# The causal triangle of an attention kernel, added by VectorE where TensorE added it with matmuls

## The chip, the cores and the metric

One NeuronCore of one Trainium2 chip runs the whole program; the seven other cores are idle. The metric is the device time of one execution in microseconds (us). The kernel before takes 2070.18 us, the median of three runs (2068.84 to 2073.34).

## What is computed

The reference passes eight sequences of 512 tokens with 256 channels through two layers. Layer one is a local attention (44 fixed offsets for each token), layer two a causal attention, and a mixture of experts follows each. Only the causal attention is touched by the change. Cut to what matters:

```python
Q = split_heads(x @ Wq + bq)      # 16 heads of 16 channels
K = split_heads(x @ Wk + bk)
V = split_heads(x @ Wv + bv)
scores = jnp.einsum('bhqd,bhkd->bhqk', Q, K) / jnp.sqrt(jnp.float32(D_HEAD))
causal = jnp.tril(jnp.ones((T, T), dtype=bool))
scores = jnp.where(causal, scores, -jnp.inf)
attn = jax.nn.softmax(scores, axis=-1)
out = jnp.einsum('bhqk,bhkd->bhqd', attn, V)
```

## The kernel before, in words

**Calls and the planner.** The work is cut into calls: A (local attention of one sequence), B (causal attention of one sequence) and F (experts, sixteen calls). A and B calls alternate after the first two A, and each F call runs beside the attention call after its own. Every call is a list of phases, and a phase is a list of blocks, each on one engine with a cost in us and needs (`local_phases`, `causal_phases`, `expert_phases`, L127 to L279). `ordered` (L391) is a list scheduler that runs when the kernel is built: it always takes the block that can start first, and the one with the longest way behind it where two tie. The result is a fixed order of instructions for each of the five engines, and `play` (L501) writes it out. A block is never broken up by another. So a changed cost or a new block in `causal_phases` can change the order of everything.

**Banks.** PSUM has eight banks. A and B calls share banks 0 to 3 in rotation and bank 4 for sums that are held; F calls rotate through banks 5 to 7. A fill may start when the reader of the fill before it in that bank is done (`fills_of` L365, `bank_free` L737).

**A causal call.** Q and K are each split into three bf16 parts that are stacked along the contraction (`q_st`, `k_st`, 96 rows), so that one bf16 matmul gives the scores. This takes a write to DRAM and a read back ("stacks"). Then, for each of the 16 heads:

- *Raw scores, S* (`raw_scores` L1596). Three fills hold four query tiles i of 128 queries: i = 3 (512 keys), i = 2 and i = 0 (384 and 128 keys), i = 1 (256 keys). For each tile TensorE multiplies q by k (L1603) and then adds the triangle of the diagonal block with a 128-column matmul of the identity and `causal` (L1605). VectorE takes the negated maximum of each tile with a `tensor_reduce` (L1287): 64 tiles in a call, 512 in all. After eight heads `mx` (L1295 to L1298) splits the maxima in three bf16 parts, `mT` turns them, and they go through DRAM into rows 96 to 98 of `q_st`.
- *Turned scores, ST* (`turned_scores` L1609). Four heads make a group, and a step is one of its four key tiles k. TensorE multiplies k by q with the maxima subtracted (L1619, 512, 384, 256 or 128 columns), then adds the turned triangle to the first 128 of these columns with a matmul of the identity and `causal_T` (L1621). `SHARE` (L75) says how heads share a bank: one head in a fill for k = 0 and 1, two for k = 2, four for k = 3, so 44 fills in a call, 352 in all, and 64 triangle matmuls in a call, 512 in all. ScalarE reads each fill with one exponential (L1050) into `p_T`, which holds two steps, so the exponential of step n waits for PV of step n-2.
- *PV* (`weigh_values` L1625, L1638) multiplies the exponentials with the values and a column of ones.

In the order of `causal_phases` the maxima of the first eight heads and two more heads come ahead of any ST. The S fills of the other six heads are laced with the ST fills of the first six steps. The other ST steps stand alone on the attention side.

```python
nc.tensor.matmul(ps[:, at:at + (i + 1) * P], q_st[0:K, h, i * P:(i + 1) * P],
                 k_st[0:K, h, 0:(i + 1) * P], start=True, stop=False, skip_group_check=True)
ins = nc.tensor.matmul(ps[:, at + i * P:at + (i + 1) * P], ident_b[:], causal[:],
                       start=False, stop=True, skip_group_check=True)
```

**Engines in the same queue.** VectorE also makes the 88 products of every A call (L1231), norms (stats, L1163 to L1170; xn, L1176), the ranking of the experts (L1317 to L1346), the sums of the experts (L1373, L1378) and the close of an F call (L1395, L1400). ScalarE also reads the expert matmuls (L1085, L1069, L1102).

## Time and profile before

| | before |
|---|---|
| median of three runs | 2070.18 us |
| the profiled execution | 2066.49 us |
| its span, first to last instruction | 2064.5 us |
| mean granted TensorE clock | 0.939 of 2.4 GHz |
| PE busy (modelled) | 1770.7 us, 86% |
| VectorE (DVE) busy | 1299.9 us, 63% |
| ScalarE (ACT) busy | 809.0 us, 39% |

Each row of a group names the line, the engine, what is written from what, and how often. The duration of a matmul in these rows runs until its last result is modelled to have left the array, so the next one starts well before its end: the distance from start to start is what an instruction takes of TensorE's time. The chain is the work that ended last, followed back from the end of the program; only time on it can shorten the run directly. The share in a query of a stretch is a share of that stretch.

### The profile page before, as it was taken

The numbers are of one execution on the slowest core, as the hardware profiler recorded it, in microseconds if no ns is written. First come the engines' busy times: TensorE is split into PE (matmuls) and PEld (weight loads), VectorE is DVE, ScalarE is ACT, GpSimd is POOL, SyncE is SP. The second block draws the span as 40 slices with busy tenths as digits, with TensorE's granted clock in tenths as the row PEclk, the third lists the DMA queues.
The fourth block names the chain that finished last, engine by engine and source line by source line (L and its number), as shares of the span: only waits on it lengthen the run. The fifth ranks groups of instructions, "written<-read, shape, count | busy, mean of one in ns | idle before, by whom it ended". The sixth has DMA issues, their size and how long they took to land.

```text
span 2064.5 us, 29256 instructions
## 1 busy us (share of the span) xinstructions
PE 1770.7 (86%) x11259; PEld 932.0 (45%) x11312; DVE 1299.9 (63%) x3090; ACT 809.0 (39%) x1473; POOL 118.9 (6%) x155
## 2 busy tenths in 40 slices
PE   4589779869998799988999789988998979898976
PEld 1243544335443554435453454535554436445443
DVE  6859563874669556686558746595565774745533
ACT  1123326323443344433453334533444334353533
POOL 1010100001000100002000010001000010000000
PEclk9799989989999899999999989998999989899889
DMA  9110240024000240004200132002500013204000
GB/s 293 69 68 22 107 151 2 22 99 138 22 22 22 107 151 8 17 22 187 72 22 22 74 134 52 22 22 100 157 2 22 22 73 122 74 2 124 3 10 11
DMA packets 47840, 137.88 MB, mean 67 GB/s; under 512 B 6184, under 2 KB 18856, under 8 KB 42920
## 3 DMA queue, kind: packets, MB, share of 16 engines
q1 hardware_dynamic: 47704, 136.02, 20.1%
q8 instruction: 91, 1.49, 0.3%
q14 instruction: 45, 0.37, 0.1%
HBM read 80.79 MB, written 46.04 MB: 61 GB/s over the span
## 4 chain that ended last, share of the span: by engine, by line
PE 61%; DVE 24%; issue 6%; ACT 5%; DMA 2%; POOL 1%; SPq 0%; POOLq 0%; DVEq 0%; ACTq 0%
PE bank L1448 24%; DVE arena_AB L1231 10%; PE bank L1731 5%; PE bank L1716 5%; PE bank L1536 4%; DVE arena_AB L1287 4%; PE bank L1638 3%; PE bank L1619 3%; PE bank L1550 3%; PE bank L1469 2%; PE bank L1603 2%; PE bank L1571 2%; PE bank L1456 1%; PE bank L1481 1%; PE bank L1621 1%
## 5 line engine op out<-in xcount | busy, mean ns | idle before, releaser
L1231 DVE TENSOR_TENSOR arena_AB<-qT,kT 128x512 f32<-128x512 f32 x704 | 428.2, 682 | 11.9 <-ACT kT L987 6.0
L1448 PE MATMUL bank<-arena_F,kept 128*128 128x512 f32 (+1 forms) x544 | 265.1, 614 | 22.7 <-ACT cont_hi L1075 10.1
L1287 DVE TENSOR_REDUCE arena_AB<-bank 128x1 f32<-128x512 f32 (+3 forms) x512 | 217.5, 482 | 79.7 <-PE bank L1605 76.2
L1536 PE MATMUL bank<-arena_AB,slot_w 128*32 128x512 f32 x1408 | 201.5, 621 | 43.9 <-DVE arena_AB L1231 41.4
L1085 ACT ACTIVATE arena_F<-bank,kept 128x512 f32<-128x512 f32 x256 | 169.1, 690 | 163.5 <-PE bank L1448 160.5
L1050 ACT ACTIVATE arena_AB<-bank 128x512 f32<-128x512 f32 (+1 forms) x352 | 180.7, 573 | 108.0 <-PE bank L1621 106.4
L1448 PEld LDWEIGHTS bank<-arena_F,kept 128*128 128x128 f32 (+1 forms) x544 | 93.4, 189 | 131.0 <-issue 86.5
L1603 PE MATMUL bank<-arena_AB 96*128 96x512 bf16 (+3 forms) x512 | 137.2, 320 | 14.0 <-DVE arena_AB L1287 8.5
L1448 PE MATMUL bank<-cont_hi,we 128*128 128x512 f32 x256 | 128.2, 501 | 23.8 <-DVE arena_F L1373 19.4
L1619 PE MATMUL bank<-arena_AB 99*128 99x256 bf16 (+3 forms) x512 | 131.3, 308 | 9.7 <-DMA arena_AB<-maxima 8.5
L1716 PE MATMUL bank<-arena_F,kept 128*64 128x512 f32 x512 | 130.2, 630 | 8.6 <-DVE arena_F L1373 5.6
L1448 PE MATMUL bank<-xnT,kept 128*128 128x512 f32 x256 | 124.7, 626 | 2.2 <-ACT xnT L969 1.7
L1731 PE MATMUL bank<-kept,arena_F 128*128 128x256 f32 x512 | 117.1, 382 | 2.5 <-ACT arena_F L1102 2.5
L1550 PE MATMUL bank<-kept,arena_AB 128*128 128x128 f32 x512 | 76.0, 305 | 43.1 <-DVE oN L1205 24.5
L1373 DVE SCALAR_TENSOR_TENSOR arena_F<-bank,kept,arena_F 128x512 f32<-128x512 f32 x64 | 47.9, 749 | 93.6 <-PE bank L1716 93.4
L1448 PE MATMUL bank<-cont_lo,we 128*128 128x512 f32 x256 | 106.6, 417 | 0.0
L1731 PEld LDWEIGHTS bank<-kept,arena_F 128*128 128x128 f32 x512 | 94.9, 189 | 23.3 <-ACT arena_F L1102 9.2
L1605 PE MATMUL bank<-causal_b,ident_b 128*128 128x128 bf16 x512 | 102.2, 230 | 0.0
L1536 PEld LDWEIGHTS bank<-arena_AB,slot_w 128*32 128x32 f32 x1408 | 35.2, 110 | 146.7 <-DVE arena_AB L1231 105.4
L1621 PE MATMUL bank<-causal_T,ident_b 128*128 128x128 bf16 x512 | 99.5, 222 | 0.0
L1008 ACT COPY arena_AB<-bank 128x512 f32<-128x512 f32 x128 | 68.2, 594 | 78.2 <-PE bank L1550 78.0
L1386 DVE TENSOR_TENSOR arena_F<-bank,kept 128x512 f32<-128x512 f32 x32 | 22.1, 692 | 121.3 <-PE bank L1731 121.3
(191 smaller groups left out, 2507.2 us busy)
## 6 DMA issues: line engine op xcount, KB each, us to landing
arena_AB<-band SPq DMA_DIRECT2D x32, 1344.0 KB, 6.3
arena_AB<-stacks SPq DMA_DIRECT2D x64, 384.0 KB, 8.7
stacks<-arena_AB SPq DMA_DIRECT2D x48, 256.0 KB, 2.9
band<-arena_AB SPq DMA_DIRECT2D x32, 328.0 KB, 2.2
stacks<-xnT SPq DMA_DIRECT2D x32, 256.0 KB, 2.6
band<-kT SPq DMA_DIRECT2D x4, 1352.0 KB, 21.8
v<-V SPq DMA_DIRECT2D x8, 576.0 KB
stacks<-xn SPq DMA_DIRECT2D x16, 256.0 KB, 3.1
```

Source lines behind the costliest of these rows:

```text
L1050: nc.scalar.activation(p_T[:, n % RS, cols[0]:cols[-1] + 1, 0:w], ps[:, 0:len(cols) * w].rearrange("p (c q) -> p c q", c=len(cols)), ACT.E ...
L1085: nc.scalar.activation(hid[:, n % RH, :], ps[:], ACT.Relu, bias=c("be1", n, 1)).then_inc(read, 1)
L1231: nc.vector.tensor_tensor(prod[n % RD], qT[:, hf, :], kT[:, hf, at:at + T], ALU.mult).then_inc(sem["A"]["prod_made"], 1)
L1287: ins = nc.vector.tensor_reduce(neg_max[:, n, i:i + 1], ps[:, at:at + (i + 1) * P], AX, ALU.max, negate=True)
L1448: ins = nc.tensor.matmul(out(ps), w, x, start=n == 0, stop=n == len(pairs) - 1)
L1536: ins = nc.tensor.matmul(ps[HS * col:HS * (col + 1), :], slot_w[:, slot(n), :], prod[n % RD], start=False, stop=r == 3, skip_group_check=True)
L1550: ins = nc.tensor.transpose(ps[:, (h % 4) * P:(h % 4 + 1) * P], band[:, i % 2, NEAR - 1:BW, h], ident)
L1603: nc.tensor.matmul(ps[:, at:at + (i + 1) * P], q_st[0:K, h, i * P:(i + 1) * P], k_st[0:K, h, 0:(i + 1) * P], start=True, stop=False, skip_ ...
L1619: nc.tensor.matmul(ps[:, at * w:(at + 1) * w], k_st[0:K + 3, h, k * P:(k + 1) * P], q_st[0:K + 3, h, k * P:T], start=True, stop=False, ski ...
L1621: ins = nc.tensor.matmul(ps[:, at * w:at * w + P], ident_b[:], causal_T[:], start=False, stop=True, skip_group_check=True)
L1716: ins = nc.tensor.matmul(ps[M * e:M * (e + 1), :], we2[:, 2 * n + e, k, :], hid[:, (4 * n + 2 * e + k) % RH, :], start=k == 0, stop=k == 1)
L1731: ins = nc.tensor.matmul(ps[:, i * D:(i + 1) * D], t_moe[:, k, at:at + P], dec_w[:, k, :], start=k == 0, stop=k == KF - 1)
```

## The change

Both triangles are added by VectorE. For the raw scores, `tensor_reduce` becomes `tensor_tensor_reduce`: it adds the score tile in PSUM and a mask, scales by -1, writes the result back over the tile in PSUM and gives the minimum in `neg_max`. The mask tile `causal` is widened from 128 to 512 columns (zeros, then the triangle), so that the last (i+1)*128 columns of it fit each tile. For the turned scores, each of the 44 fills of a call gets a VectorE `tensor_tensor` that adds `causal_T` in PSUM to the first 128 columns of each of its heads, between the matmul and the exponential. ScalarE waits for this add (`st_masked`) in place of the full bank. The 1024 triangle matmuls go.

The planner's table follows: PE costs of S from (0.3, 0.45, 0.25) to (0.22, 0.23, 0.12), of ST from (0.3, 0.25, 0.35, 0.5) to (0.22, 0.17, 0.23, 0.24), a new DVE block in ST of (0.22, 0.22, 0.36, 0.64), DVE costs of S as they were. The value tiles `V`, `V_b`, `v_96`, `v_near` are packed to 17 columns for each head (16 values and the one) where 32 stood; a matmul still loads 32 columns, of which the last 15 are now those of the next head and end in rows that nothing reads.

```diff
+HV = HD + 1
+VW = H * HV + HS - HV
+BIG = 3.0e38
-PACK_S = [("pair_sel", (E // 2) * P), ("slot_mask", 4 * HS), ("se", J), ("is_slot", NG * P), ("ahead", T), ("causal", P),
+PACK_S = [("pair_sel", (E // 2) * P), ("slot_mask", 4 * HS), ("se", J), ("is_slot", NG * P), ("ahead", T), ("causal", T),
+ST_FILLS = [(n, m) for n, (_, k) in enumerate(STEPS) for m in range(len(SHARE[k]))]
-        p.put(("S", h, n), ("PE", (0.3, 0.45, 0.25)[n], ("stack", h // 4, "DMA")), ("DVE", (0.62, 0.8, 0.36)[n]))
+        p.put(("S", h, n), ("PE", (0.22, 0.23, 0.12)[n], ("stack", h // 4, "DMA")), ("DVE", (0.62, 0.8, 0.36)[n]))
+        p.put(("ST", n, m), ("PE", (0.22, 0.17, 0.23, 0.24)[k], ("mT", g // 2, "DMA")), ("DVE", (0.22, 0.22, 0.36, 0.64)[k]),
+              ("ACT", (0.6, 0.5, 0.6, 0.6)[k], *([("PV", n - 2, "PE")] if n >= 2 else [])))
-        V = sb("V", [P, TT, H, HS])
+        V = sb("V", [P, TT, VW])
-        causal = sb("causal_b", [P, P], bf16)
+        causal = sb("causal_b", [P, T], bf16)
-                        act.wait_ge(*bank_full(u, ("ST", g, k, m)))
+                        act.wait_ge(*nth(u, "st_masked", ST_FILLS.index((n, m)) + 1))
                         for i, at in MAX_FILLS[name[2]]:
-                            ins = nc.vector.tensor_reduce(neg_max[:, n, i:i + 1], ps[:, at:at + (i + 1) * P], AX,
-                                                          ALU.max, negate=True)
+                            s = ps[:, at:at + (i + 1) * P]
+                            ins = nc.vector.tensor_tensor_reduce(
+                                out=s, in0=s, in1=causal[:, (TT - 1 - i) * P:T], scale=-1.0, scalar=BIG, op0=ALU.add,
+                                op1=ALU.min, accum_out=neg_max[:, n, i:i + 1])
+                    elif kind == "ST":
+                        heads_ = len(SHARE[k][m])
+                        dve.wait_ge(*bank_full(u, ("ST", g, k, m)))
+                        ps, _ = place(u, ("ST", g, k, m))
+                        s = ps[:, 0:heads_ * (T - k * P)].rearrange("p (c q) -> p c q", c=heads_)[:, :, 0:P]
+                        nc.vector.tensor_tensor(s, s, causal_T[:].unsqueeze(1).broadcast_to([P, heads_, P]), ALU.add
+                                                ).then_inc(sem["B"]["st_masked"], 1)
-                        ins = nc.tensor.matmul(ps[:, at + i * P:at + (i + 1) * P], ident_b[:], causal[:],
-                                               start=False, stop=True, skip_group_check=True)
-                        ins = nc.tensor.matmul(ps[:, at * w:at * w + P], ident_b[:], causal_T[:],
-                                               start=False, stop=True, skip_group_check=True)
```

## Rows read from the trace of the kernel before

**Rows 1.** The page: busy time of the engines, and the chain by engine and line.
```profile
PE 1770.7 (86%) x11259; PEld 932.0 (45%) x11312; DVE 1299.9 (63%) x3090; ACT 809.0 (39%) x1473; POOL 118.9 (6%) x155
PE 61%; DVE 24%; issue 6%; ACT 5%; DMA 2%; POOL 1%; SPq 0%; POOLq 0%; DVEq 0%; ACTq 0%
PE bank L1448 24%; DVE arena_AB L1231 10%; PE bank L1731 5%; PE bank L1716 5%; PE bank L1536 4%; DVE arena_AB L1287 4%; PE bank L1638 3%; PE bank L1619 3%; PE bank L1550 3%; PE bank L1469 2%; PE bank L1603 2%; PE bank L1571 2%; PE bank L1456 1%; PE bank L1481 1%; PE bank L1621 1%
```

**Rows 2.** Groups by line and shape: both triangle matmuls (count, busy, mean ns).
```profile
L1605 PE MATMUL bank<-causal_b,ident_b 128*128 128x128 bf16 x512 | 102.2, 230 | 0.0
L1621 PE MATMUL bank<-causal_T,ident_b 128*128 128x128 bf16 x512 | 99.5, 222 | 0.0
```

**Rows 3.** Timeline of TensorE (start, duration, us), at the full clock, then at half.
```profile
1064.39 0.22 PE L1621 MATMUL bank<-causal_T,ident_b 128*128 128x128 bf16 x1
1064.45 0.38 PE L1619 MATMUL bank<-arena_AB 99*128 99x512 bf16 x1
...
290.15 0.31 PE L1605 MATMUL bank<-causal_b,ident_b 128*128 128x128 bf16 x1
290.25 0.42 PE L1603 MATMUL bank<-arena_AB 96*128 96x256 bf16 x1
```

**Rows 4.** Chain, stretch 1020 to 1080 us (fifth B call), by line.
```profile
by line: PE bank L1448 16.1%; PE bank L1638 13.9%; PE bank L1731 12.0%; PE bank L1619 11.0%; PE bank L1716 9.6%; ACT arena_AB L1050 7.0%; PE bank L1603 4.2%; PE bank L1621 4.0%; DMA arena_AB<-maxima 3.8%; issue 2.8%; DVE arena_F L1373 2.5%;
```

**Rows 5.** Chain, pieces in that call (start, us): first and last L1605, one run of L1050.
```profile
999.58 0.07 PE bank L1605
...
1056.98 0.06 PE bank L1605
...
1064.70 1.47 ACT arena_AB L1050 x3
```

**Rows 6.** Chain by line, stretches 280 to 400 us (first B call) and 1880 to 2000 us (last).
```profile
by line: PE bank L1448 22.5%; DVE arena_AB L1287 14.0%; DVE arena_AB L1231 9.1%; PE bank L1619 8.9%; PE bank L1638 8.6%; DMA arena_AB<-stacks 5.4%; PE bank L1716 4.0%; PE bank L1603 3.6%; PE bank L1536 3.5%; PE bank L1621 3.1%; PE bank L145
...
by line: issue 53.0%; PE bank L1448 23.7%; DVE arena_AB L1287 10.3%; PE bank L1619 9.9%; PE bank L1638 9.0%; PE bank L1716 6.3%; PE bank L1731 6.0%; PE bank L1603 5.5%; PE bank L1621 3.3%; PE bank L1605 2.1%; DVE arena_F L1395 1.3%; DVE sta
```

**Rows 7.** Groups by shape: VectorE operations that read PSUM.
```profile
L1287 DVE TENSOR_REDUCE arena_AB<-bank 128x1 f32<-128x512 f32 x128 | 87.7, 685 | 59.0 <-PE bank L1605 57.8
...
L1287 DVE TENSOR_REDUCE arena_AB<-bank 128x1 f32<-128x128 f32 x128 | 35.8, 279 | 0.0
...
L1373 DVE SCALAR_TENSOR_TENSOR arena_F<-bank,kept,arena_F 128x512 f32<-128x512 f32 x64 | 47.9, 749 | 93.6 <-PE bank L1716 93.4
...
L1386 DVE TENSOR_TENSOR arena_F<-bank,kept 128x512 f32<-128x512 f32 x32 | 22.1, 692 | 121.3 <-PE bank L1731 121.3
```

**Rows 8.** Timeline of VectorE: reductions back to back, and two short instructions behind one another.
```profile
1010.43 0.19 DVE L1338 TENSOR_REDUCE arena_F<-arena_F 128x4 f32<-128x32 f32 x1
1010.65 0.18 DVE L1339 RECIPROCAL arena_F<-arena_F 128x4 f32<-128x4 f32 x1
...
1011.86 3.93 DVE L1287 TENSOR_REDUCE arena_AB<-bank 128x1 f32<-128x384 f32 x10
```

**Rows 9.** Chain by line, stretch 999 to 1020 us.
```profile
by line: DVE arena_AB L1287 62.2%; DMA arena_AB<-stacks 32.9%; DVE x_third L1367 5.4%; DVE arena_F L1373 3.6%; issue 3.1%; DVE cont_lo L1360 2.8%; DVE arena_F L1330 2.1%; DVE arena_F L1331 2.1%; DVE arena_F L1332 2.1%; PE bank L1603 1.9%; D
```

**Rows 10.** Waits over the whole run: engine, line, what it waited for, us, times, longest.
```profile
ACT arena_AB L1050 <- PE bank L1621: 106.4, 85, 4.8
```

**Rows 11.** Windows: us, then PE, PEld, DVE, ACT, POOL busy (instructions), granted clock, DMA share, GB/s.
```profile
1000.00:1020.00 20.00, 17.22 (x110) 9.36 (x109) 19.25 (x56) 8.83 (x16) 0.00 (x0) 1.00 0.33 77
...
1060.00:1080.00 20.00, 17.71 (x176) 8.11 (x175) 10.73 (x42) 15.01 (x31) 3.04 (x3) 1.00 0.17 56
```

**Rows 12.** Timeline of VectorE in the last steps of the same call.
```profile
1061.64 1.67 DVE L1395 SCALAR_TENSOR_TENSOR arena_F<-arena_F,mv_F,kept 128x256 f32<-128x256 f32 x4 [0.88 <-POOL rstd_F L906]
1063.34 1.67 DVE L1400 SCALAR_TENSOR_TENSOR x_third<-arena_F,rstd_F,x_third 128x256 f32<-128x256 f32 x4
...
1065.05 1.41 DVE L1163 BATCH_NORM_STATS2 stats_F<-x_second 128x6 f32<-128x256 f32 x4
```

**Rows 13.** Timeline of VectorE in the setup: a cast of 512 columns.
```profile
12.49 0.43 DVE L1143 CAST ahead<-arena_F 128x512 bf16<-128x512 f32 x1
```

60 lines of the change are left out of this document (30 added, 30 removed).

## The prediction

> **What bounds the kernel now.** I read the page first. TensorE is busy for 86% of the span, VectorE for 63% [rows 1]. A busy share says little here: the duration of a matmul overlaps the next one. So I read the chain next. It puts 61% of the span on TensorE, 24% on VectorE and 5% on ScalarE [rows 1]. No single engine is the bound; the bound changes from stretch to stretch, and the change moves work from one engine that is often on the chain to another that sometimes is. So the question has to be put to the stretches of a B call. I take the fifth, 999 to 1080 us, since the middle calls look alike.
>
> From 999 to 1020 us the chain runs through VectorE: 62.2% of the stretch is the maxima, most of the rest other VectorE work and the wait for the stacks [rows 9], and the window says 19.25 of 20 us busy for VectorE at 17.22 for TensorE [rows 11]. From 1020 to 1080 us TensorE carries it: L1448, L1638, L1731, L1619 and L1716 make 63% [rows 4]. In the last 20 us TensorE (17.71) and ScalarE (15.01) are both close to full and VectorE is at 10.73 [rows 11].
>
> **The triangle matmuls that go.** They look large: 102.2 and 99.5 us of busy time [rows 2]. But a row of 220 ns is no 220 ns of TensorE's time. At the full clock the next matmul starts 0.06 us after the start of a triangle, at half clock 0.10 us [rows 3]. 1024 of them are 61 us of TensorE's stream, not 202. And of these 61 only what lies on the chain comes off by itself. In the fifth call L1621 has 4.0% of 60 us, 2.4 us [rows 4], and L1605 has 19 pieces of 0.06 to 0.07 us, 1.2 us [rows 5]; 3.6 us in all. Six middle calls make 21.6 us. The first call has 3.1% of 120 us for L1621, 3.7 us, and I give it the same 1.2 us for L1605; the last has 3.3 and 2.1%, 6.5 us [rows 6]. Sum 33 us. The rest, 28 us, falls where VectorE or a DMA is late anyway.
>
> The Trainium skill ("TensorE: Matmul & The Clock Gate", Back-to-back issue gap) has two prices for a 128-column matmul: 56 ns alone, and about 81 ns in a stream where each matmul has a weight load of its own. This stream is of the second kind, yet the trace shows the first. By the second, the stream would be 83 us, an estimate from that page, and more would be on the chain; the trace decides against it.
>
> **The maxima with the triangle added.** Each of the 512 reductions becomes an operation with two inputs, an output over the tile and a minimum. No row shows this operation. Nearest rows: a two-input add from PSUM of 512 columns takes 692 ns, the reduction 685, so a second input costs 7 ns; the three-operand form takes 749, 57 ns more than the two-operand one [rows 7]. Above that, a separate small instruction behind each one would cost the distance of two short ones, 0.22 us [rows 8]. Below nothing is excluded, since it streams as many columns. I take 57 ns, because the new form also carries two operators and one output more than the add, and keep 0 and 0.22. How many lie on the chain: L1287 has 4% of 2064.5 us, 83 us [rows 1], at 0.39 us each back to back (ten in 3.93 [rows 8]), 211 of them. 211 x 0.057 = 12 us. The other 301 hide behind TensorE, and cost as much each if that cover is gone.
>
> A rule speaks against this edit. The Trainium skill ("VectorE: DVE Perf Modes", Two Vector instructions with no wait between them) says that an operation that also writes out its accumulator is two instructions, the main one and an accumulator read. The trace of before has none, so it can't be weighed here; if it holds and the read is not overlapped, the third rival below is what it looks like.
>
> **The masks of the turned scores.** 352 new adds on VectorE. From the rows, a PSUM operation of 128 columns takes 279 ns and one of 512 takes 685 to 692 [rows 7]; 256 lie between. They write to PSUM, which no VectorE row does; I take the same price, between nothing less and the 57 ns of an extra operand more. In a call 32 adds of one head, 8 of two and 4 of four are about 32 x 0.28 + 8 x 0.42 + 4 x 0.69 = 15 us, 120 us in all, and VectorE goes from 63 to about 70% busy. Most of it is covered by TensorE's work. What isn't: where the chain steps from TensorE into an exponential, it now steps through VectorE first. In the fifth call L1050 has 7.0% of 60 us, 4.2 us [rows 4], some eight exponentials in runs of up to three [rows 5], so about five entries. Five entries in eight calls at 0.28 us and 0.05 us for the second handover (my assumption; the rows don't part it) are 13 us. Bounds: 0, if the exponentials had slack everywhere (ScalarE waited 106.4 us for L1621 in 85 waits, the longest 4.8 us, so it is mostly early [rows 10]), and 40 x 0.69 = 28 us.
>
> What queues behind the new waits: VectorE now waits for the full bank of each ST fill, and the maxima and the experts' sums stand behind it; ScalarE waits for VectorE, and the experts' reads stand behind it; the bank of a fill is held longer by the add, and TensorE's next fill but three stands behind that.
>
> **Setup and layout.** The wider triangle is one more cast of 512 columns where 128 stood, at most 0.43 us [rows 13], and some more bytes of a load: 1 us. The values packed to 17 columns change no count of instructions and no count of loaded columns; fewer bytes are shifted, beside other work. Nothing.
>
> **The sum.** -33 + 12 + 13 + 1 = -7 us. On the profiled execution, 2066.49 us, that gives 2059.5; this execution is 3.7 us under the median of the three runs, so against the median it is 2063 us. Its own range, from the bounds above without a queue: 2051 to 2077.
>
> **Rivals.**
> 1. *TensorE's whole stream counts.* The planner makes the order anew, and can fill the room with other calls' matmuls, so that all 61 us come off and the adds hide. For it: 61% of the chain is TensorE, and the new PE costs are nearer to the distances in rows 3. Against it: 999 to 1020 us is VectorE's [rows 9], and no TensorE work can shorten it. -61 + 12 + 1 = -48: 2022 us.
> 2. *Masks behind long blocks, slower than before.* VectorE's queue is in order and a planner's block is not broken up. In the last steps of a call the close of an F call is 3.4 us in one piece and the next norm follows with 1.4 and more [rows 12]. Masks for a little over two groups, at 3.8 us a group, take VectorE from 10.7 to over 19 of 20 us [rows 11], and `p_T` holds only two steps, so ScalarE and PV soon stand. One whole close in front of a mask is 3.5 us in a call: 8 x 3.5 = 28, 2091 us. It decides the sign from 7 / 8 = 0.9 us a call. Against it: part of this place is now a wait for the maxima's DMA, and TensorE can take experts' work in between.
> 3. *The new reduction is dear.* At 0.22 us instead of 0.057: 211 x 0.163 = 34 us more, 2097 us. It streams at one column a cycle in this; at half that rate it would be 211 x 0.39 = 83 us more, which I give almost nothing.
> 4. *The change doesn't do what it says*: the triangles were hidden, and so are the adds. 2070 us. It is part of the forecast's own range.
>
> **Chances.** Forecast 0.36 (of it faster 0.24, same 0.09, slower 0.03); rival 1 0.20; rival 2 0.27 (slower 0.25, same 0.02); rival 3 0.12 (slower 0.10, same 0.02); 0.05 for neither, same or slower. A measurement of this kernel can tell about 0.2%, 4 us, from no change. Faster 0.45, same 0.14, slower 0.41. Both signs are likely. The range reaches to rival 1 and most of rivals 2 and 3: 2022 to 2095.
>
> **What would show it.** Term one: TensorE's count falls by 1024 and the L1619 rows start 0.06 us closer; the granted clock stays near 0.94. Term two: the new operation's 512-column row at 740 ns, and 999 to 1020 us some 2 us longer; at 900 ns it is rival 3. Term three: the adds at 0.28 us, and in the chain one short VectorE piece ahead of each exponential. Rival 2 shows as ScalarE's exponentials waiting for the adds for 1 us and more at a time, while VectorE's rows in front are L1395, L1400 and L1163. The prediction is wrong if the planner's new order moves whole phases: then the B call and the A call after it change in length with no term of mine in them.

## The result, and the profile after

The changed kernel takes 2122.88 us (median of 4 runs, 2120.38 to 2125.19), the kernel before 2069.51 in the same sessions: ratio 1.0255, 95% interval 1.0236 to 1.0275, some 53 us slower. The forecast was 2063 us, with a range of 2022 to 2095. The sign was wrong, and the time lies outside the range.

From the page of the profiled execution: busy times, the granted clock over 40 slices (in tenths of full speed), and the head of the chain (compare [rows 1]):

```profile
span 2121.2 us, 28082 instructions
PE 1769.5 (83%) x10237; PEld 874.3 (41%) x10288; DVE 1419.1 (67%) x3954; ACT 804.3 (38%) x1473; POOL 118.2 (6%) x155
...
PEclk9799979989799998999999999998998999798888
...
PE 56%; DVE 32%; issue 5%; ACT 4%; DMA 2%; POOL 1%; SPq 0%; POOLq 0%; DVEq 0%; ACTq 0%
PE bank L1468 23%; DVE arena_AB L1240 15%; DVE bank L1297 5%; PE bank L1747 5%; PE bank L1732 5%; PE bank L1654 4%; PE bank L1637 3%; PE bank L1556 3%; PE bank L1570 2%; PE bank L1489 2%; PE bank L1591 2%; PE bank L1476 2%; PE bank L1623 1%; DVE stats_F L1172 1%; PE bank L1501 1%
```

TensorE lost 1024 instructions and has less of the chain, 56 for 61%. VectorE took it: 32 for 24%. It gained 864 rows, 352 masks and 512 accumulator reads. The largest gain is that of the products of the local attention (L1240, was L1231), 15% for 10%, which the change does not touch. Added up over the whole chain, the masks hold 17 us of it, the maxima 123 us for 79. The mean granted clock fell from 0.939 to 0.905.

The groups by shape (busy, mean ns | idle before, releaser), to be laid beside [rows 2, 7]. L1297 are the new maxima, L1308 the masks:

```profile
L1297 DVE CUSTOM_DVE_ANT_0 bank<-bank,causal_b 128x512 f32<-128x512 f32 x128 | 90.6, 708 | 22.8 <-PE bank L1623 22.4
L1297 DVE CUSTOM_DVE_ANT_0 bank<-bank,causal_b 128x128 f32<-128x128 f32 x128 | 42.2, 330 | 0.0
L1297 DVE DVE_READ_ACCUMULATOR2_ANT arena_AB<- 128x1 f32 x512 | 71.8, 140 | 0.0
L1308 DVE TENSOR_TENSOR bank<-bank,causal_T 128x128 f32<-128x128 f32 x256 | 70.0, 304 | 53.9 <-PE bank L1637 52.8
L1308 DVE TENSOR_TENSOR bank<-bank,causal_T 128x256 f32<-128x256 f32 x64 | 25.9, 432 | 15.6 <-PE bank L1637 15.4
L1308 DVE TENSOR_TENSOR bank<-bank,causal_T 128x512 f32<-128x512 f32 x32 | 22.4, 699 | 22.1 <-PE bank L1637 21.9
```

The masks have about the durations that were forecast (304, 432 and 699 ns for 280, 420 and 690), 118 us of busy time against 120. The new maximum is two rows: the pass (708 ns for 512 columns, 685 before) and a read of the accumulator of 140 ns, which mostly runs beside the next row. What counts is the distance of heads back to back: 1.79 us for the four tiles of a head, 1.60 before, so 0.05 us a tile.

The waits over the whole run (us, times, longest), to be laid beside [rows 10]:

```profile
DVE bank L1308 <- PE bank L1637: 90.1, 90, 3.8
ACT arena_AB L1059 <- DVE bank L1308: 76.1, 105, 3.1
PEld bank L1623 <- DVE arena_AB L1297: 67.7, 130, 2.5
PEld bank L1637 <- ACT arena_AB L1059: 33.2, 63, 1.7
```

ScalarE now waits for VectorE, and TensorE's weight loads for the raw scores wait 67.7 us for a bank that VectorE frees, 29.9 before.

The same call as [rows 11] in windows (us, then PE, PEld, DVE, ACT, POOL busy, granted clock, DMA share, GB/s), 21 us later than before:

```profile
1020.00:1040.00 20.00, 17.64 (x74) 8.20 (x73) 18.84 (x77) 8.51 (x14) 0.00 (x0) 0.83 0.27 68
...
1080.00:1100.00 20.00, 16.27 (x96) 5.90 (x95) 17.93 (x72) 11.59 (x24) 3.03 (x3) 0.83 0.18 56
```

In the last steps, 1080 to 1100, VectorE is at 17.93 of 20 us where it was at 10.73 [rows 11], and TensorE falls from 17.71 to 16.27 at a lower clock: 0.83 of full speed is a mixture of the two levels, 1.2 and 2.4 GHz, where both windows in [rows 11] show 1.00.

What stands in front of a mask can be seen earlier in the call. TensorE, VectorE, then ScalarE:

```profile
1058.96 0.33 PE L1637 MATMUL bank<-arena_AB 99*128 99x384 bf16 x1
...
1058.84 0.75 DVE L1393 SCALAR_TENSOR_TENSOR arena_F<-bank,kept,arena_F 128x512 f32<-128x512 f32 x1 [1.48 <-PE bank L1732]
1059.62 0.69 DVE L1398 TENSOR_TENSOR arena_F<-arena_F 128x512 f32<-128x512 f32 x1
1060.23 0.69 DVE L1297 CUSTOM_DVE_ANT_0 bank<-bank,causal_b 128x512 f32<-128x512 f32 x1
...
1060.84 0.33 DVE L1308 TENSOR_TENSOR bank<-bank,causal_T 128x128 f32<-128x128 f32 x1
...
1061.20 0.49 ACT L1059 ACTIVATE arena_AB<-bank 128x384 f32<-128x384 f32 x1 [2.60 <-DVE bank L1308]
```

ScalarE had been idle for 2.60 us before the exponential at 1061.20. The scores of this fill were ready at 1059.29, so 1.9 us lie between them and their exponential. The mask, 0.33 us long, stood behind a maximum, and that behind the sums of an expert's output (L1393, L1398), the first of which had itself waited 1.48 us for TensorE. VectorE takes its blocks in the order of its queue.

The place that rival 2 named is not among these. At the step whose exponential the close of an experts' call would hold (step 7), after's masks start 0.04 us behind their fill in seven of the eight calls. Over the 352 masks, the times between a full bank and the start of its mask add up to 170 us; 45 of them VectorE spent on maxima, 27 on other masks, and 22 on the second half of a close.

### The profile page after: what moved, and what is told of

It reads as the page before. It is cut to its first block, busy times and chain, and to the rows that moved or that the text cites. A ratio compares the mean times of both kernels' runs of the same rounds, so it can differ in the third digit from the quotient of the medians.

```text
span 2121.2 us, 28082 instructions
## 1 busy us (share of the span) xinstructions
PE 1769.5 (83%) x10237; PEld 874.3 (41%) x10288; DVE 1419.1 (67%) x3954; ACT 804.3 (38%) x1473; POOL 118.2 (6%) x155
## 4 chain that ended last, share of the span: by engine, by line
PE 56%; DVE 32%; issue 5%; ACT 4%; DMA 2%; POOL 1%; SPq 0%; POOLq 0%; DVEq 0%; ACTq 0%
PE bank L1468 23%; DVE arena_AB L1240 15%; DVE bank L1297 5%; PE bank L1747 5%; PE bank L1732 5%; PE bank L1654 4%; PE bank L1637 3%; PE bank L1556 3%; PE bank L1570 2%; PE bank L1489 2%; PE bank L1591 2%; PE bank L1476 2%; PE bank L1623 1%; DVE stats_F L1172 1%; PE bank L1501 1%
## 5 line engine op out<-in xcount | busy, mean ns | idle before, releaser
L1240 DVE TENSOR_TENSOR arena_AB<-qT,kT 128x512 f32<-128x512 f32 x704 | 428.6, 683 | 18.2 <-PE bank L1556 10.3
L1556 PE MATMUL bank<-arena_AB,slot_w 128*32 128x512 f32 x1408 | 212.3, 650 | 65.7 <-DVE arena_AB L1240 52.8
L1297 DVE CUSTOM_DVE_ANT_0 bank<-bank,causal_b 128x512 f32<-128x512 f32 (+3 forms) x512 | 237.2, 517 | 27.3 <-PE bank L1623 26.4
L1308 DVE TENSOR_TENSOR bank<-bank,causal_T 128x128 f32<-128x128 f32 (+2 forms) x352 | 117.9, 363 | 91.7 <-PE bank L1637 90.1
L1468 PE MATMUL bank<-cont_hi,we 128*128 128x512 f32 x256 | 136.2, 532 | 35.6 <-DVE arena_F L1339 32.6
L1637 PE MATMUL bank<-arena_AB 99*128 99x256 bf16 (+3 forms) x512 | 121.9, 326 | 14.1 <-ACT arena_AB L1059 12.3
L1732 PE MATMUL bank<-arena_F,kept 128*64 128x512 f32 x512 | 125.5, 610 | 4.8 <-ACT arena_F L1094 3.2
L1654 PE MATMUL bank<-arena_AB,V_b 128*32 128x512 f32 (+3 forms) x1024 | 108.2, 498 | 10.6 <-ACT arena_AB L1059 9.3
L1393 DVE SCALAR_TENSOR_TENSOR arena_F<-bank,kept,arena_F 128x512 f32<-128x512 f32 x64 | 47.9, 749 | 93.5 <-PE bank L1732 88.7
L1623 PEld LDWEIGHTS bank<-arena_AB 96*128 96x128 bf16 x512 | 45.4, 105 | 130.3 <-DVE arena_AB L1297 67.7
L1006 ACT ACTIVATE arena_AB<-bank,kept 128x512 f32<-128x512 f32 (+1 forms) x48 | 32.9, 686 | 172.9 <-PE bank L1556 172.9
L915 POOL TENSOR_TENSOR rstd_F<-var_eps_F,minus_half 128x4 f32<-128x4 f32 x32 | 33.8, 1057 | 1146.2 <-DVE var_eps_F L1179 1146.2
```

Of the source, the lines that this page charges most:

```text
L1240: nc.vector.tensor_tensor(prod[n % RD], qT[:, hf, :], kT[:, hf, at:at + T], ALU.mult).then_inc(sem["A"]["prod_made"], 1)
L1297: ins = nc.vector.tensor_tensor_reduce(out=s, in0=s, in1=causal[:, (TT - 1 - i) * P:T], scale=-1.0, scalar=BIG, op0=ALU.add, op1=ALU.min, ...
L1308: nc.vector.tensor_tensor(s, s, causal_T[:].unsqueeze(1).broadcast_to([P, heads_, P]), ALU.add).then_inc(sem["B"]["st_masked"], 1)
L1468: ins = nc.tensor.matmul(out(ps), w, x, start=n == 0, stop=n == len(pairs) - 1)
L1556: ins = nc.tensor.matmul(ps[HS * col:HS * (col + 1), :], slot_w[:, slot(n), :], prod[n % RD], start=False, stop=r == 3, skip_group_check=True)
L1623: ins = nc.tensor.matmul(ps[:, at:at + (i + 1) * P], q_st[0:K, h, i * P:(i + 1) * P], k_st[0:K, h, 0:(i + 1) * P], start=True, stop=True)
```

## The experiments

Besides the layout, two things were changed at once: the work, and the planner's table, from which the order of all blocks on all engines is worked out anew. Where a kernel below is said to be in before's or after's order, TensorE's, ScalarE's and VectorE's blocks stand in exactly that sequence; in before's order the masks are put into VectorE's queue at the planned end of their matmul. All times are ratios to the kernel before with 95% intervals; 0.01 is 20.7 us. All of them have the packed values and the wide triangle, but for no_tri.

### Order against work

Kernel *layout_only*: triangles by TensorE, plain maxima, before's table; of the change only the packed values and the wide triangle remain. Against after:

```diff
-                            ins = nc.vector.tensor_tensor_reduce(
...
+                            ins = nc.vector.tensor_reduce(neg_max[:, n, i:i + 1], ps[:, at:at + (i + 1) * P], AX,
+                                                          ALU.max, negate=True)
...
+                        ins = nc.tensor.matmul(ps[:, at * w:at * w + P], ident_b[:], causal_T[:],
+                                               start=False, stop=True, skip_group_check=True)
```

> Only the packing of the values in 17 columns and the wider triangle of zeros are kept; triangles by TensorE, maxima, planner's costs and order are those of before, block for block. All theories but one: 2070 us, within 4. The layout theory (loads of 32 columns that now begin at multiples of 17, shifted copies of another shape) would show 2080 or more here.

Measured: 0.9983 (0.9959 to 1.0007), 2067 us. The layout costs nothing.

Kernel *order_only*: after's table and order with before's work, triangles by TensorE and plain maxima. The planned mask block stays in the table, and does nothing. Of its edit against after:

```diff
...
+                    elif kind == "ST":
+                        pass
...
```

> The planner's order is that of after, block for block; the work is that of before (triangles by TensorE, plain maxima, the planned blocks of the masks are empty). Order theory (the new order moves phases: experts' projections slid in between the turned scores, products late): most of the 53 us, 2105 to 2125. Work theory (the adds and the wait behind VectorE's queue cost it, whatever the order): 2060 to 2080.

Measured: 1.0155 (1.0117 to 1.0193), 2100 us, +32.

Kernel *both_before_order*: the whole work of after, before's order. Against after (the table is that of before):

```diff
...
+    for t, x in masks:
+        at = sum(s < t for s in starts)
+        order["DVE"].insert(at, x)
+        starts.insert(at, t - 1e-9)
```

> The work is that of after in full; the order of every block on every engine is that of before, with the masks put into VectorE's queue at the planned end of their matmul. Order theory: 2063 to 2075, near the forecast. Work theory: 2105 to 2130. If both carry half: 2085 to 2100.

Measured: 1.0312 (1.0280 to 1.0344), 2132 us, +65.

So order and work each cost time alone, and do not add: 32 and 65 against 53 for both. With the heavy work, after's order is the better of the two, by some 10 us.

Kernel *raw_before_order* (maxima with the triangle, turned scores as before) and *turned_before_order* (the other half) part the work. The first against after:

```diff
-                        ins = nc.tensor.matmul(ps[:, at * w:(at + 1) * w], k_st[0:K + 3, h, k * P:(k + 1) * P],
-                                               q_st[0:K + 3, h, k * P:T], start=True, stop=True)
+                        nc.tensor.matmul(ps[:, at * w:(at + 1) * w], k_st[0:K + 3, h, k * P:(k + 1) * P],
+                                         q_st[0:K + 3, h, k * P:T], start=True, stop=False, skip_group_check=True)
+                        ins = nc.tensor.matmul(ps[:, at * w:at * w + P], ident_b[:], causal_T[:],
+                                               start=False, stop=True, skip_group_check=True)
```

> Half of the work in before's order: the maxima of the raw scores add the triangle themselves, the turned scores keep the triangle matmul and have no mask. By the forecast's own terms: triangles on the chain of this half 1.2 us in 8 calls, 10 off, and 12 for the new reduction: 2072. By the trace of after (ten heads of raw scores 1.8 us longer in a call, 8 calls, nothing back): 2084. Work theory with the masks as the cause: this one stays within 15 us of before. If it has most of the 53, the reduction is the cause.

Measured: 1.0060 (1.0032 to 1.0087), 2083 us, +12.

> The other half of the work in before's order: the turned scores' triangle is added by VectorE ahead of the exponential, the raw scores keep their triangle matmul and the plain maxima. If the halves add up, this one takes the full work's 2132 less the 13 of the raw half: 2110 to 2125. If the two halves load VectorE together and only their sum hurts, it is well under that: 2075 to 2095.

Measured: 1.0220 (1.0187 to 1.0253), 2114 us, +46. The halves make 58, the whole work 65. In before's order the masks of the turned scores are the larger part by far.

Kernel *raw_after_order*: the same edit with after's table, the planned mask block empty as in order_only.

> After's order, block for block; the maxima add the triangle themselves, the turned scores have their triangle by TensorE and no mask. The order alone was 2100, all of after is 2123. If the raw half costs the 13 us that it costs in before's order: 2113, and 10 are left for the masks of the turned scores. If the masks carry it in this order too: 2100 to 2105.

Measured: 1.0212 (1.0182 to 1.0242), 2113 us, +44. Over its order alone the raw half costs 12 here too. Changed one after another in this sequence, after's 53 are: order 32, raw scores 12, masks 9. In the other sequence they are: work 65, order -12. The shares hold for the sequence alone.

### What the triangles were worth

Kernel *no_tri*: before, all 1024 triangle matmuls left out, and the causal mask with them.

```diff
-                        ins = nc.tensor.matmul(ps[:, at + i * P:at + (i + 1) * P], ident_b[:], causal[:],
-                                               start=False, stop=True, skip_group_check=True)
```

> Before, in its own order, with all 1024 triangle matmuls left out and nothing in their place (the causal mask is left out of the computation). It prices what the change can gain at most on TensorE. By the forecast's first term: 33 off, 2036. If the whole stream counts: 61 off, 2008. If what is freed only turns into waits for VectorE and the maxima: 2055 to 2069.

Measured: 0.9940 (0.9921 to 0.9958), 2057 us, -12. The page of this kernel:

```profile
PE 1739.6 (85%) x10235; PEld 872.9 (43%) x10288; DVE 1299.4 (63%) x3090; ACT 807.1 (39%) x1473; POOL 118.9 (6%) x155
...
PE 58%; DVE 27%; issue 6%; ACT 6%; DMA 2%; POOL 1%; SPq 0%; POOLq 0%; DVEq 0%; ACTq 0%
```

Of the 33 us that the chain put on triangles a third came off. In the chain the other engines gained: VectorE has 27 for 24%, ScalarE 6 for 5. Taking the times at which no matmul runs from the first maximum of a B call to its last exponential, and adding up the eight calls, TensorE stands still 62.6 us here and 46.2 before.

And the granted clock is lower: 0.925 in this profile, 0.921 to 0.926 in all nine executions, where 63 of before have 0.932 to 0.944. The call of [rows 11] in this kernel, where before shows 1.00 in both windows:

```profile
992.00:1012.00 20.00, 16.25 (x75) 7.86 (x74) 18.17 (x49) 8.50 (x15) 0.00 (x0) 0.91 0.38 90
...
1052.00:1072.00 20.00, 17.67 (x145) 6.69 (x137) 12.94 (x51) 14.20 (x31) 3.04 (x3) 0.91 0.19 56
```

Within the eight B calls TensorE is at the half level, 1.2 GHz, for 103 us here and 50 before. A fill of 512 columns with its triangle takes 0.27 us of TensorE from start to start at the full level and 0.53 at the half. What this costs can be estimated from before alone. Its 63 executions spent 230 to 283 us at the half level (twice what the mean clock lacks to 1, times the span), and with each us of it they took 0.31 us longer, give or take 0.05. No_tri spends 316 us there on average, 58 more than before and outside that range; by this estimate that is 18 us. With before's clock it would then have gained some 30 us, close to the 33 of the chain. No run holds the clock still, so this stays an estimate, but it is as good an account of the missing 21 us as the next engine's share.

### What a step between fill and exponential costs

These keep before's work in full (triangles by TensorE) and before's order, and add one small thing in the mask's place.

Kernel *hop_vector*: VectorE adds one column per head, and the exponential waits for it.

```diff
+                        dve.wait_ge(*bank_full(u, ("ST", g, k, m)))
+                        s = ps[:, 0:heads_ * (T - k * P)].rearrange("p (c q) -> p c q", c=heads_)[:, :, 0:1]
+                        nc.vector.tensor_tensor(s, s, causal_T[:, 0:1].unsqueeze(1).broadcast_to([P, heads_, 1]), ALU.add
+                                                ).then_inc(sem["B"]["st_masked"], 1)
```

> All work and order of before, triangles by TensorE; one thing is added: between each fill of the turned scores and its exponential VectorE adds one column per head (the triangle's first column, which is masked already), in the place where the mask would stand. Duration theory (118 us of masks are too much for VectorE): 352 adds of one column cost little, 2070 to 2085. Handover theory (a bank now passes two engines one after the other, and waits for its turn in VectorE's queue): most of the turned half's loss, 2105 to 2125.

Measured: 1.0128 (1.0094 to 1.0162), 2096 us, +26.

Kernel *hop_gpsimd*: the same turn between fill and exponential, taken by a one-column memset of a scratch tile on GpSimd.

> As the one before, but the step between the fill and its exponential is a one-column memset on GpSimd, which has little else to do in this stretch. Queue theory (what costs is the turn in VectorE's queue, behind maxima, closes and norms): 2068 to 2080. Latency theory (two handovers in place of one, four banks in the ring): as much as with VectorE, 2100 or more.

Measured: 1.0005 (0.9981 to 1.0028), 2069 us, nothing. Two handovers instead of one, and a bank of the ring held longer by them, are free; the turn on VectorE is not. The memset is short and GpSimd idle:

```profile
L985 POOL MEMSET hop<- 128x1 f32 x352 | 35.7, 101 | 764.8 <-PE bank L1654 762.9
```

Kernels *stop_only* and *turn_only* part the two directions. In the first VectorE waits for the fill and nobody for VectorE; in the second the other way round. Both do a one-column memset of a scratch tile. *stop_only*:

```diff
+                        dve.wait_ge(*bank_full(u, ("ST", g, k, m)))
+                        nc.vector.memset(hop[:, at:at + 1], 0.0).then_inc(sem["B"]["st_masked"], 1)
```

*turn_only*:

```diff
+                        nc.vector.memset(hop[:, at:at + 1], 0.0).then_inc(sem["B"]["st_masked"], 1)
...
                         act.wait_ge(*bank_full(u, ("ST", g, k, m)))
+                        act.wait_ge(*nth(u, "st_masked", ST_FILLS.index((n, m)) + 1))
```

> Before's work and order. VectorE waits for each fill of the turned scores in the mask's place and then sets one column of a scratch tile; the exponential does not wait for VectorE. So VectorE's queue stops at the fills, and nobody waits for its turn. If the stop of VectorE's queue is what costs (what stands behind it: maxima, closes, norms, stacks' readers): 2088 to 2098, like the one-column adds (2096). If ScalarE's wait for VectorE's turn is what costs: 2067 to 2075.

Measured: 0.9998 (0.9974 to 1.0021), 2069 us, nothing.

> The mirror of the one before: the one-column memset does not wait for the fill, the exponential waits for the fill and for the memset. VectorE's queue never stops for it, but ScalarE waits until VectorE has got that far. If ScalarE's wait for its turn is the cause: 2088 to 2098. If the stop is: 2067 to 2076. If it takes both (each engine hands its delay to the other, round after round): both kernels stay under 2080.

Measured: 1.0106 (1.0076 to 1.0137), 2092 us, +22. It is ScalarE's wait for its turn in VectorE's queue, with no mask and some 20 us of VectorE time. VectorE, ScalarE and TensorE of this kernel in the call that began at 1004, at steps 7 and 8:

```profile
1068.27 1.67 DVE L1427 SCALAR_TENSOR_TENSOR arena_F<-arena_F,mv_F,kept 128x256 f32<-128x256 f32 x4 [0.86 <-POOL rstd_F L932]
1069.98 1.67 DVE L1432 SCALAR_TENSOR_TENSOR x_third<-arena_F,rstd_F,x_third 128x256 f32<-128x256 f32 x4
1071.71 0.42 DVE L1190 BATCH_NORM_STATS2 stats_F<-x_second 128x6 f32<-128x256 f32 x1
1071.72 0.08 DVE L1321 MEMSET hop<- 128x1 f32 x3
...
1071.89 1.57 ACT L1077 ACTIVATE arena_AB<-bank 128x512 f32<-128x512 f32 x3 [3.60 <-DVE hop L1321]
...
1070.70 0.39 PE L1651 MATMUL bank<-arena_AB 99*128 99x512 bf16 x1 [1.52 <-DMA arena_AB<-maxima]
```

The close of an experts' call takes 3.4 us in two rows, then come the memsets of 0.08, and the next exponential of ScalarE, idle for 3.60 us. The scores of step 7 had been ready at 1068.62, so this exponential was held for 3.3 us by its turn. The other two of the row were not: their matmuls, of step 8, start at 1070.70 and 1070.99, since TensorE had waited for the DMA that brings the maxima. Before has that wait too, 1.75 us at this place.

From the end of a fill's last matmul to the start of its exponential, added up over all 352 fills, it is 127 us before, 252 in turn_only, 276 in hop_vector, 385 in turned_before_order, 399 in both_before_order and 414 in after.

Kernel *load_only*: a maximum over a constant in SBUF, which waits for nothing and holds nobody.

```diff
+                        nc.vector.tensor_reduce(hop[:, at:at + 1], causal[:, 0:(256, 384, 0, 512)[len(SHARE[k][m]) - 1]], AX,
+                                                ALU.max).then_inc(sem["B"]["st_masked"], 1)
```

> Before's work and order, and in the mask's place a maximum over 256, 384 or 512 columns of a constant in SBUF, which takes about as long as the mask (0.3 to 0.6 us) and waits for nothing and is waited for by nobody. It prices the 118 us of VectorE alone. By the forecast (hidden beside TensorE's work): 2070 to 2076. If VectorE's time counts in the stretch of the raw and turned scores together: 2080 to 2095.

Measured: 1.0055 (1.0034 to 1.0075), 2081 us, +11. It is a little heavier than the masks, 145 us:

```profile
L1320 DVE TENSOR_REDUCE hop<-causal_b 128x1 f32<-128x256 bf16 (+2 forms) x352 | 145.1, 458 | 0.4
```

How the delay grows within a call: end of some exponentials after the call's first maximum, mean of the three middle calls, worked out from the rows of the timelines (the calls that begin at 757, 1000 and 1242 in before). The first column is before, the others are the delay against it, in us. Each is one execution. The same ends move by 0.1 to 1.4 us in layout_only, stop_only and hop_gpsimd, which cost nothing; and the profiled executions of load_only and turn_only are 7 and 6 us under their medians.

```
step, head(s)    before   load_only  turn_only  hop_vector  hop_split  turned  both
ST 0, first       32.6      0.6        0.1        1.0         0.6       0.7     2.8
ST 5, last        59.3      1.5        1.0        1.8         1.4       2.0     4.4
ST 7              63.6      3.2        4.2        5.3         2.8       6.1     8.5
ST 8, first       66.4      1.9        1.9        3.0         2.0       3.9     6.2
ST 9, last        69.9      1.9        2.5        3.6         4.2       4.8     7.2
ST 11             72.6      1.6        3.1        4.6         5.7       6.8     9.4
ST 15             79.9      1.7        3.1        5.0         6.1       7.4    10.0
```

(both is both_before_order, turned is turned_before_order, hop_split is told below.) Three things stand in it. The raw scores give 2.8 us ahead of the first exponential, in the last column alone. Steps 0 to 5 add little. Steps 6 to 15, which have no raw scores beside them, add the most. The close costs some 3 us at step 7, and 2.3 of them are won back at step 8, whose matmuls wait for the maxima's DMA with or without it.

### Can the queue be rearranged?

Kernel *hop_vector_first*: as hop_vector, with each column add whose turn would come inside a block of 1.2 us or more put ahead of that block. *both_first*: the same for the whole work.

```diff
         at = sum(s < t for s in starts)
+        while at and ends[at - 1] > t and order["DVE"][at - 1][1][0] != "ST":
+            at -= 1
```

> As the one-column adds on VectorE before (1.013, 2096), the same order on TensorE and ScalarE; in VectorE's queue each add whose turn would come inside a block of 1.2 us or more (closes, norm statistics, the norm itself, an output, experts' sums of 1.6) now stands ahead of that block. Theory of long blocks (rival 2 of the forecast): most of the 25 us comes back, 2072 to 2082. Theory of the short ones (80 masks stand straight behind a maximum of the raw scores, and every wait for a fill stops VectorE's queue): it stays at 2090 to 2100, or grows, since VectorE now idles ahead of the long blocks.

Measured: 1.0263 (1.0237 to 1.0289), 2124 us, +54.

> The full work of after in before's order (2132), with the masks ahead of the long blocks as in the one before. Long blocks: 2100 to 2112. Short ones and load: 2125 to 2140.

Measured: 1.0433 (1.0401 to 1.0464), 2157 us, +90.

Both are worse by 25 to 28 us than with the masks where they were. As I read it, the close now stands behind a mask that waits for its fill, and still ahead of the next masks; no run parts this further.

Kernel *hop_vector_split*: the close in four pieces and the norm statistics in two, and the next masks moved up between the pieces of the close.

```diff
                         for i in range(TT):
+                            if i == 2:
+                                yield "close", 1
                             ins = nc.vector.scalar_tensor_tensor(
```

> The one-column adds on VectorE in before's order (2096); the only change is in VectorE's queue: a close of an experts' call is now four pieces of 0.85 us and the norm statistics two, and the next masks stand between the pieces, where a whole close of 3.4 us stood ahead of them. If the whole blocks are what ScalarE waits for in the last steps (3.63 us once in each middle call): about 8 times 2.5 us less, 2072 to 2082. If that wait is covered by the work that TensorE has at hand, and the loss comes from where VectorE waits for TensorE (3.54 us behind the decoder's matmuls): 2090 to 2100.

Measured: 1.0153 (1.0132 to 1.0173), 2100 us, +32, against 1.0128 whole: nothing won. *both_split*:

> The full work of after in before's order (2132), with the closes and the statistics in pieces and the next masks between them. Whole blocks: 2105 to 2118. Otherwise: 2125 to 2138.

Measured: 1.0291 (1.0265 to 1.0316), 2131 us, +60, against 1.0312: nothing that can be measured. ScalarE in steps 7 and 8, first of hop_vector, then of hop_vector_split:

```profile
1071.55 0.60 ACT L1075 ACTIVATE arena_AB<-bank 128x512 f32<-128x512 f32 x1 [3.63 <-DVE bank L1322]
```

```profile
1076.42 0.60 ACT L1090 ACTIVATE arena_AB<-bank 128x512 f32<-128x512 f32 x1 [1.56 <-DVE bank L1338]
1078.24 0.60 ACT L1090 ACTIVATE arena_AB<-bank 128x512 f32<-128x512 f32 x1 [1.22 <-DVE bank L1338]
1079.03 0.60 ACT L1090 ACTIVATE arena_AB<-bank 128x512 f32<-128x512 f32 x1 [0.20 <-DVE bank L1338]
1081.45 1.08 ACT L1090 ACTIVATE arena_AB<-bank 128x512 f32<-128x512 f32 x2 [1.82 <-DVE bank L1338]
```

The wait of 3.63 us, and one of 0.49 behind it, have become four of 4.80 together. Step 7 comes earlier (2.8 for 5.3 in the table), and by step 9 the delay is back. VectorE's rows show why:

```profile
1078.91 0.87 DVE L1455 SCALAR_TENSOR_TENSOR x_third<-arena_F,rstd_F,x_third 128x256 f32<-128x256 f32 x2
1079.81 1.41 DVE L1203 BATCH_NORM_STATS2 stats_F<-x_second 128x6 f32<-128x256 f32 x4
1081.25 0.36 DVE L1338 TENSOR_TENSOR bank<-bank,causal_T 128x1 f32<-128x1 f32 x4
```

The last piece of the close and all of the statistics still stand in one row of 2.3 us, and four masks wait behind them. Over the run VectorE spent 21 us on closes and 14 on statistics while a filled bank waited for its column add in hop_vector, 19 and 32 in hop_vector_split; all such waits add up to 102 and 111 us. So the pieces moved the wait from one block to the next, and a queue without long blocks ahead of masks was not tested.

### What the order does

Kernel *order_pe*: before's work and no mask block; only TensorE's costs in the planner's table are those of after, for the raw scores as shown and for the turned ones in the same way.

```diff
-        p.put(("S", h, n), ("PE", (0.3, 0.45, 0.25)[n], ("stack", h // 4, "DMA")), ("DVE", (0.62, 0.8, 0.36)[n]))
+        p.put(("S", h, n), ("PE", (0.22, 0.23, 0.12)[n], ("stack", h // 4, "DMA")), ("DVE", (0.62, 0.8, 0.36)[n]))
```

> Work of before, no mask; of the planner's table only TensorE's costs are those of after (0.22, 0.23, 0.12 for a head's raw scores; 0.22, 0.17, 0.23, 0.24 for the turned ones). It parts the 31 us of the order: if the lower costs of TensorE make it, 2090 to 2105; if the masks' planned blocks on VectorE make it, 2065 to 2078.

Measured: 1.0115 (1.0090 to 1.0140), 2093 us, +24.

Kernel *after_oldpe*: after, with TensorE's costs of before in the table, again for both.

```diff
-        p.put(("ST", n, m), ("PE", (0.22, 0.17, 0.23, 0.24)[k], ("mT", g // 2, "DMA")), ("DVE", (0.22, 0.22, 0.36, 0.64)[k]),
+        p.put(("ST", n, m), ("PE", (0.3, 0.25, 0.35, 0.5)[k], ("mT", g // 2, "DMA")), ("DVE", (0.22, 0.22, 0.36, 0.64)[k]),
```

> Work of after in full with its masks planned as in after (0.22 to 0.64 us on VectorE), but TensorE's costs of before in the planner's table. If the lower TensorE costs are what hurts in the new order: 2095 to 2110, better than after's 2123. If the order only matters through the masks' blocks: within 8 of 2123. If leaving before's order of TensorE is all that helped: about 2132.

Measured: 1.0305 (1.0282 to 1.0328), 2133 us, +63, as much as the whole work in before's order. The lower costs of TensorE are bad for the light work and good for the heavy one; no price can be put on a table apart from its work.

What moved can be seen in order_only. TensorE in the last steps of the call that begins at 1016; L1459 is the experts' next encoder, L1632 the triangle of the turned scores:

```profile
1090.22 0.22 PE L1632 MATMUL bank<-causal_T,ident_b 128*128 128x128 bf16 x1
1090.28 3.65 PE L1459 MATMUL bank<-arena_F,kept 128*128 128x512 f32 x8
1093.86 0.64 PE L1649 MATMUL bank<-arena_AB,V_b 128*32 128x256 f32 x8
...
1096.23 1.93 PE L1459 MATMUL bank<-arena_F,kept 128*128 128x512 f32 x4
```

and in before, where the encoder's first matmuls come behind the call's last weighing of values (L1638):

```profile
1078.65 0.43 PE L1638 MATMUL bank<-arena_AB,V_b 128*32 128x128 f32 x8 [0.18 <-ACT arena_AB L1050]
1079.17 1.96 PE L1448 MATMUL bank<-arena_F,kept 128*128 128x512 f32 x4
```

So 5.6 us of the encoder fall between the last steps of the B call, instead of behind them, beside the products of the next local attention. It is so in more than this call: in five of order_only's calls the encoder takes 5.3 us within steps 11 to 15, and these steps last 12.5 us; in the same calls of before they last 8 to 10 with 0 to 2 us of encoder. After has 4.9 us of it there, in five calls too. The sums over eight B calls, from first maximum to last exponential, agree: 632 us before, 671 in order_only, 696 in after, 697 in both_before_order; and products take 14% of order_only's chain (10% before). That the encoder would have cost less beside the products is my reading; no run moves it alone. In order_pe it lies elsewhere: its B calls sum to 636, and each of the first five stretches between one call's last exponential and the next call's first maximum grew by 4 to 8 us. No run of its own asks what happens there, and it stays open. Its time at the half level is 43 us longer than before's, 13 us by the estimate above.

## Why the prediction was wrong, point by point

*The triangles, -33: too large.* The counts and distances were right, TensorE lost 1024 instructions. no_tri measured -12, interval -9 to -16. The step that failed is "what lies on the chain comes off by itself", and with it "the granted clock stays near 0.94". I had subtracted the 28 us off the chain and took the 33 on it as pure gain, without asking for each call what is late next. By [rows 11] ScalarE was at 15.01 of 20 us in the very stretch where I took 2.4 us a call. And the clock fell to 0.925, which by the estimate is 18 of the missing 21 us. Which of the two it was stays open.

*The maxima, +12: right in each, their number open.* 57 ns an operation was forecast, 0.05 us measured. Ahead of the first exponential a head is 0.19 us longer, ten heads some 2 us, eight calls 15. The raw half cost 12 us with its share of the triangles already taken off. By my terms this half should have cost 1 to 2. One account is that "211 of 512 are on the chain, the other 301 hide" failed, since VectorE's share of the chain was 24% and grew. The other is the clock: raw_before_order is 37 us longer at the half level than before, 11 us by the estimate. Nothing parts them.

The rule of the Trainium skill ("VectorE: DVE Perf Modes", Two Vector instructions with no wait between them) holds here: the trace has the second instruction, 512 rows of 140 ns. Rival 3, which would have made it dear, did not come: the read lies beside the next row. The price that the Trainium skill ("TensorE: Matmul & The Clock Gate", Back-to-back issue gap) gives for a 128-column matmul with its weight load, 81 ns, stays contradicted by the triangles' 0.06 us.

*The masks, +13 with bounds of 0 and 28: the failed term.* Durations and count were right (118 us for 120). Priced was one mask in front of one exponential, 40 times. With its triangles taken off, my terms gave this half -9. Measured is +46 in before's order, and +9 on top of the rest in after's. The 46 can be laid out as about 22 for ScalarE's turn in VectorE's queue (turn_only), about 11 for VectorE's extra time (load_only, somewhat heavier than the masks), some 6 us less for this half's triangles if no_tri parts evenly, and so about 19 for what only comes with all of it together: perhaps the mask's length, which now lies in the loop from fill to exponential to the next fill, and the clock, whose lower mean is 14 of the 46 us by the estimate and 7 of turn_only's 22. That last part is a remainder, not a measurement. The text listed who queues behind whom, and then put no number on it; the bound of 28 was of one mask without its queue.

*Rival 2, 2091, slower: right engine and right queue, and its size by luck.* It put 28 us on masks behind a close, and hop_vector measures 26. turn_only shows an exponential held for 3.3 us behind a close of 3.4, in five of the eight calls. But the 3 us at the close are mostly won back, because the step behind it waits for the maxima's DMA anyway (the text had that as its argument against). What stays are several delays of 0.5 to 1 us in steps 6 to 11. And in after itself the close does not stand at step 7. Whether other long blocks carry the loss is open, since the pieces of hop_vector_split still leave one of 2.3 us. I gave this 0.27, and priced it without the load of VectorE and the raw scores, which come on top.

*Layout and setup, nothing and +1: right.* layout_only is 0.9983.

*The planner's order, no term at all.* The prediction named it as what would make it wrong, and that is what happened: alone it is +32, at the same clock but for 4 us of the estimate, and the largest piece of after's 53 in that sequence. With the whole work in place the same order is some 10 better than before's.

Rival 1 (the planner fills the room, -48) did not come: after is 53 slower, and with all triangles gone and nothing added the gain is 12. That run keeps before's order, so it doesn't say what a planner would make of the room.

*Four slips in the working, none of which decides.* "Most of the rest" of [rows 9] is not the wait for the stacks: the view counts a piece in full where it only reaches into the window, and cut to the window that wait is 0.7% and VectorE 94%. The own range of 2051 to 2077 varies the masks alone and leaves out the bounds 0 and 0.22 of the maxima. The chances of faster add up to 0.44, not 0.45. And the call at 1000 is the fourth B call, not the fifth.

No version beat the kernel before in any arrangement that keeps the mask. With 12 us measured for the triangles, and 11 for VectorE's time alone (a little heavier than the masks), next to nothing is left for one on VectorE. That holds for the orders that were run.

## What to carry to other kernels

A step put on an engine that takes its blocks in order costs its turn as well as its length: measure the turn by itself, with an operation that does nothing (here 22 us for memsets of 0.06 us, and nothing measurable on GpSimd, which is busy for 6%). What the chain holds of an operation need not come off with it (33 us held, 12 measured); ask what is late next before subtracting it, and compare the granted clock before blaming the next engine. Where a planner orders the work from a table of costs, a changed table is a change of its own: run the new order with the old work and the old order with the new work before believing either.

## What was unexpected in the hardware

A tensor-tensor reduction with a 512-column output in PSUM takes 708 ns, and the accumulator read behind it 140 ns, of which only some 0.05 us a tile show in the distance of operations back to back. 352 stops of VectorE for fills that it does not need cost nothing (stop_only), though they hold its queue. And TensorE's clock goes down with the change: in the windows of the call it was at 1.00 before and at 0.83 in the two windows of after in which TensorE was busy for 17.64 and 16.27 of 20 us. Within the eight B calls TensorE is at the half level for 50 us before, 103 in no_tri, 156 in both_before_order and 175 in after, and it stands still there for 46, 63, 115 and 84 us. After has 134 us more of the half level than before over its four executions. By before's 0.31 us for each that is 41 of the 53 us, but it lies far outside the range in which the 0.31 was found, and after's own four executions give 0.15, so 20. No run here parts it. order_only loses 32 us with only 14 us more of the half level, so most of its loss is not the clock.
